# Layer 0's attention heads: masks added by VectorE, two banks for turned blocks, value products in the ring of pairs

## The reference, cut to what matters

```python
content = jnp.einsum('bihd,bjhd->bhij', q + u_bias, k)
pos = jnp.einsum('bihd,jhd->bhij', q + v_bias, p)
pos = _relative_shift(pos)
attn = jax.nn.softmax((content + pos) * scale, axis=-1)
head = jnp.einsum('bhij,bjhd->bihd', attn, v).reshape(B, S, Dm)
```

## Time and profile before

| what | value |
|---|---|
| median of 3 runs | 2649.91 us (2646.68 to 2653.76) |
| the profiled execution | 2652.1 us, its span 2650.3 us |
| setup and projections | 0 to 235 us of the span |
| layer 0's heads | 235 to 1376 us |
| layer 0's merge and experts | 1376 to 2086 us |
| layer 1's heads | 2086 to 2476 us |
| tail | 2476 us to the end |
| share of the span busy | PE 86%, PEld 50%, DVE 61%, ACT 50%, POOL 27% |

### The profile page before, as it was taken

How to read it: one execution, slowest core, us unless ns; L and a number is a source line. 1 busy time by engine, 2 the same in 40 slices (tenths; PEclk the granted TensorE clock), 3 DMA queues, 4 the chain that set the end, 5 groups by cost and what they waited for, 6 DMA issues and landing times. The chain is left out here.

```text
span 2650.3 us, 51680 instructions
## 1 busy us (share of the span) xinstructions
PE 2286.8 (86%) x17274; PEld 1338.0 (50%) x17274; DVE 1618.7 (61%) x2775; ACT 1324.9 (50%) x2282; POOL 704.4 (27%) x573
## 2 busy tenths in 40 slices
PE   3663999999999999999975999999999299999577
PEld 2331777777777777777742444444444144444232
DVE  3894777777777777777744243443442478888354
ACT  1220666566666565656642454455544055555454
POOL 1444444444444444443401122212222100000000
PEclk9775999999999999999986999999999599999799
DMA  4443111111111111111102112122211222222221
GB/s 167 141 143 108 31 37 37 37 37 37 36 33 33 34 33 33 37 37 37 33 22 67 60 40 76 60 87 87 79 36 64 69 72 84 83 83 75 86 77 40
DMA packets 94926, 163.61 MB, mean 62 GB/s; under 512 B 18120, under 2 KB 44242, under 8 KB 93586
## 3 DMA queue, kind: packets, MB, share of 16 engines
q1 hardware_dynamic: 94866, 162.82, 19.5%
HBM read 102.37 MB, written 60.41 MB: 61 GB/s over the span
## 5 line engine op out<-in xcount | busy, mean ns | idle before, releaser
L1112 ACT ACTIVATE prob<-pair,neg_max_h 128x640 f32<-128x640 f32 x512 | 407.0, 795 | 391.0 <-DVE neg_max_h L1012 391.0
L1012 DVE TENSOR_REDUCE neg_max_h<-pair 128x1 f32<-128x640 f32 x512 | 419.5, 819 | 276.2 <-PE pair L936 271.1
L889 PE MATMUL turn<-ident,prob 128*128 128x128 f32 x2048 | 504.9, 278 | 16.1 <-ACT prob_t L1120 9.0
L889 PEld LDWEIGHTS turn<-ident,prob 128*128 128x128 f32 x2048 | 287.3, 140 | 125.5 <-issue 95.6
L1120 ACT COPY prob_t<-turn 128x512 f32<-128x512 f32 x512 | 297.7, 581 | 95.6 <-PE turn L889 93.9
L1588 PE MATMUL pair<-hid,down_w 128*128 128x512 f32 x640 | 307.1, 626 | 29.4 <-DVE moe L1373 25.2
L1072 POOL TENSOR_TENSOR a_full<-rot_c,rot_s 128x512 f32<-128x512 f32 x128 | 162.5, 1269 | 613.0 <-DVE rot_s L1002 613.0
L1891 ACT ACTIVATE prob_h<-pair 128x256 f32<-128x256 f32 (+3 forms) x512 | 205.7, 436 | 195.2 <-PE pair L1778 188.5
L1514 ACT ACTIVATE hid<-pair,up_b 128x512 f32<-128x512 f32 x320 | 200.8, 690 | 124.9 <-PE pair L1568 124.6
L1019 DVE TENSOR_TENSOR prob<-prob 128x128 f32<-128x128 f32 x512 | 256.7, 501 | 0.7 <-ACT prob L1112 0.7
L1830 DVE TENSOR_REDUCE row_max<-pair 128x1 f32<-128x128 f32 (+3 forms) x512 | 221.4, 485 | 56.4 <-PE pair L1757 52.0
(11 more groups left out here) (265 smaller groups left out, 4322.6 us busy)
## 6 DMA issues: line engine op xcount, KB each, us to landing
vx_d<-vx SPq DMA_DIRECT2D x16, 1024.0 KB, 4.8
o_d<-out_sb SPq DMA_DIRECT2D x64, 256.0 KB, 2.0
w_all<-w_d SPq DMA_DIRECT2D x8, 2048.0 KB, 7.1
val<-vx_d SPq DMA_DIRECT2D x32, 256.0 KB, 6.6
val_h<-vx_d SPq DMA_DIRECT2D x32, 256.0 KB
qs_d<-part_q SPq DMA_DIRECT2D x48, 128.0 KB
ks_d<-part_k SPq DMA_DIRECT2D x48, 128.0 KB
num<-o_d SPq DMA_DIRECT2D x24, 256.0 KB
```

Of the source, the lines that this page charges most:

```text
L889: return nc.tensor.transpose(turn_bank[:, jb * P:(jb + 1) * P], prob[s % 4][:, c0:c0 + P], ident[:, :])
L1012: nc.vector.tensor_reduce(neg_max[par][:, s:s + 1], pair[:, S - (ib + 1) * P:2 * S - ib * P], AX_X, ALU.max, negate=True).then_inc(max_don ...
L1112: nc.scalar.activation(prob[s % 4][:, :], pair[:, S - (ib + 1) * P:2 * S - ib * P], ACT.Exp, bias=neg_max[par][:, s:s + 1]).then_inc(exp_d ...
```

## The change

- The two mask products per unit go away. A table `pair_mask` (128 x 1024 in f32, zero but for the masks) is built once in setup, by a memset and two copies on DVE. `dve_max` becomes one fused operation, `tensor_tensor_reduce`: it adds the mask to the 640 scores, negates the sum, writes it to `prob` in SBUF, and takes the minimum of the negated sums into `neg_max`. In the program it is two instructions, the main one and one that writes the 128 x 1 result. It waits for `turned` of four units before as well, since it overwrites that tile.
- `act_exp` reads `prob` in SBUF and writes it in place, with scale -1, in place of reading the pair.
- A pair of scores is free when the fused operation is done (`max_done`), no longer when exp is.
- Turned blocks alternate between `turn_bank` and `out_bank` (`turns`); PE turns unit s once unit s-2 is copied.
- The value products of a query block take a place in the ring of pairs (`PV_SLOTS` = 3, 7, 11, 15), and DVE copies each block's 128 columns on their own (`dve_out`), in place of one copy of 512. Their place is free when that copy is done (`out_copied`). The last two rotations move one slot later (slots 9 and 12). The ring has 24 places in place of 21 (of which 20 were used).

```diff
-            ROT_SLOTS = (2, 5, 8, 11)
+            ROT_SLOTS = (2, 5, 9, 12)
+            PV_SLOTS = (3, 7, 11, 15)
...
-            RING = 21
+            RING = 24
...
                 if kind == "score":
-                    pe.wait_ge(exp_done.sem, exp_done.at(UNITS0 * group + n + 1))
+                    pe.wait_ge(max_done.sem, max_done.at(UNITS0 * group + n + 1))
+                elif kind == "pv":
+                    owner = group - 1 if n == NB - 1 else group
+                    pe.wait_ge(out_copied.sem, out_copied.at(NB * owner + n + 1))
...
-                return nc.tensor.transpose(turn_bank[:, jb * P:(jb + 1) * P], prob[s % 4][:, c0:c0 + P], ident[:, :])
+                return nc.tensor.transpose(turns[s % 2][:, jb * P:(jb + 1) * P], prob[s % 4][:, c0:c0 + P], ident[:, :])
...
-                pe.wait_ge(kept.sem, kept.at(UNITS0 * g + s))
+                pe.wait_ge(kept.sem, kept.at(UNITS0 * g + s - 1))
...
-                nc.tensor.matmul(pair[:, S - P:S], identb[:, :], mask_low, start=False, stop=True, skip_group_check=True)
-                n_up = P + 1 if ib < NB - 1 else P
-                nc.tensor.matmul(pair[:, S:S + n_up], identb[:, :], mask_up[:, 0:n_up], start=False, stop=True,
-                                 skip_group_check=True).then_inc(score_ready.sem, 1)
...
-                nc.vector.tensor_reduce(neg_max[par][:, s:s + 1], pair[:, S - (ib + 1) * P:2 * S - ib * P], AX_X,
-                                        ALU.max, negate=True).then_inc(max_done.sem, 1)
+                v.wait_ge(turned.sem, turned.at(UNITS0 * g + s - 3))
+                v.sem_inc(scores_seen, 1)
+                cols = slice(S - (ib + 1) * P, 2 * S - ib * P)
+                nc.vector.tensor_tensor_reduce(prob[s % 4][:, :], pair[:, cols], pair_mask[:, cols], -1.0, 3.0e38,
+                                               ALU.add, ALU.min, neg_max[par][:, s:s + 1]).then_inc(max_done.sem, 1)
...
-                nc.vector.tensor_copy(out_sb[:, :], out_bank[:, :]).then_inc(out_copied.sem, 1)
+                nc.vector.tensor_copy(out_sb[:, ib * P:(ib + 1) * P], pair[:, 0:P]).then_inc(out_copied.sem, 1)
...
-                nc.scalar.activation(prob[s % 4][:, :], pair[:, S - (ib + 1) * P:2 * S - ib * P], ACT.Exp,
-                                     bias=neg_max[par][:, s:s + 1]).then_inc(exp_done.sem, 1)
+                nc.scalar.activation(prob[s % 4][:, :], prob[s % 4][:, :], ACT.Exp, bias=neg_max[par][:, s:s + 1],
+                                     scale=-1.0).then_inc(exp_done.sem, 1)
```

More of the change, by code:

```diff
@@ L143, in build @@
         out_bank = ctx.enter_context(nc.psum_tensor("outsum", [P, S], F32))
+        turns = [turn_bank, out_bank]
         bank = [pairs[i // 2][:, (i % 2) * S:(i % 2 + 1) * S] for i in range(6)] + [turn_bank, out_bank]
@@ L870, in pair_free @@
                         break
+                    if kind == "pv" and not (n == NB - 1 and first(group)):
+                        break
                     at -= 3
                 if kind == "score":
-                    pe.wait_ge(exp_done.sem, exp_done.at(UNITS0 * group + n + 1))
+                    pe.wait_ge(max_done.sem, max_done.at(UNITS0 * group + n + 1))
+                elif kind == "pv":
+                    owner = group - 1 if n == NB - 1 else group
+                    pe.wait_ge(out_copied.sem, out_copied.at(NB * owner + n + 1))
                 else:
@@ L931, in pe_unit @@
                     turn_block(gt, st, 3).then_inc(turned.sem, 1)
[L932 to L937 removed]
+                nc.tensor.matmul(lo_ap, lo_low, pe_hi[:, S:S + low], start=False, stop=True, skip_group_check=True)
+                nc.tensor.matmul(up_ap, lo_up, pe_hi[:, i0:S], start=False, stop=True, skip_group_check=True
+                                 ).then_inc(score_ready.sem, 1)
             def pe_turn(pe, g, s):
@@ L956, in pe_pv @@
                     pe.wait_ge(val_loaded[par].sem, val_loaded[par].at(16 * (r + 1)))
-                    pe.wait_ge(out_copied.sem, out_copied.at(g))
                 for jb in range(NB):
                     for h in range(GH):
-                        mm = nc.tensor.matmul(out_bank[32 * h:32 * h + 32, ib * P:(ib + 1) * P], val[par][:, jb, h, :],
+                        mm = nc.tensor.matmul(pair[32 * h:32 * h + 32, 0:P], val[par][:, jb, h, :],
                                               prob_t[ib % 2][:, h, jb, :], start=(jb == 0), stop=(jb == NB - 1),
@@ L972, in pe_group @@
                         pe_rotate(pe, *nxt, h, pairs[idx % 3])
[L973 to L976, removed]
+                    if s in PV_SLOTS and not (first(g) and s < GH):
+                        ib = (PV_SLOTS.index(s) - 1) % NB
+                        idx = place["pv", ib]
+                        pair_free(pe, g, idx, nxt is not None)
+                        if ib == NB - 1:
+                            pe_pv(pe, g - 1, r - 1 if par == 0 else r, 1 - par, ib, pairs[idx % 3])
+                        else:
+                            pe_pv(pe, g, r, par, ib, pairs[idx % 3])
             def pe_all(pe):
@@ L993, in pe_all @@
                 pe_turn_max(pe, NG - 1, 1, pairs[0])
-                pe_pv(pe, NG - 1, NG // 2 - 1, 1, NB - 1)
+                pe.wait_ge(max_done.sem, max_done.at(UNITS0 * NG))
+                pe_pv(pe, NG - 1, NG // 2 - 1, 1, NB - 1, pairs[1])
             def dve_rotation(v, n, h, pair):
@@ L1040, in dve_group @@
                         dve_diag(v, gd, sd)
-                    if t == LAG + 1 and not first(g):
-                        dve_out(v, g - 1)
                     if t in ROT_SLOTS and nxt is not None:
@@ L1045, in dve_group @@
                         dve_rotation(v, nxt, h, pairs[place["rot", h] % 3])
+                    if t in PV_SLOTS and not (first(g) and t < GH):
+                        ib = (PV_SLOTS.index(t) - 1) % NB
+                        dve_out(v, g - 1 if ib == NB - 1 else g, ib, pairs[place["pv", ib] % 3])
             def dve_all(v):
@@ L1119, in act_keep @@
                 act.wait_ge(pv_done.sem, pv_done.at(NB * g + ib - 1))
-                nc.scalar.copy(prob_t[ib % 2][:, h].rearrange("p b n -> p (b n)"), turn_bank[:, :]).then_inc(kept.sem, 1)
+                nc.scalar.copy(prob_t[ib % 2][:, h].rearrange("p b n -> p (b n)"), turns[s % 2][:, :]).then_inc(kept.sem, 1)
             def act_group(act, g, par):
```

26 lines of the change are left out of this document (16 added, 10 removed).

## The result

The changed kernel takes 2528.61 us (median of 4 runs, 2522.06 to 2532.69), the kernel before 2651.01 us in the runs beside it: a ratio of 0.9545, 95% interval 0.9526 to 0.9563, or 122 us less. The forecast was 2540 us and 110 us less, in a range of 2518 to 2600. The profiled execution took 2532.68 us, 119.4 less than that of before.

A forecast was written before the change was run, and what follows sets the result against it. TensorE's list with stalls at the turn bank was taken as the bound. Per group 1.76 (masks) + 1.9 (stalls) - 0.2 (new stall) = 3.47 us, x 32 = 111, less 1.5 setup: 110 us gained, 2540 us; range 2518 to 2600.

The forecast's parts named there:

- The bound: Layer 0's heads: TensorE's list sets the pace, 34.7 us per group of 16 units, 1.9 of it stalls at the turn bank.
- Rival B: Turned blocks on TensorE: the stall isn't the bank's, so only the mask products go; 2595 us, chance 0.09.
- The masks: Mask products on TensorE: 0.11 us per unit, 1.76 per group, all on the path; 56 us gained.
- the earlier release: Ring of score pairs: a pair is free some 0.9 us earlier, at the fused operation's end; no gain counted.
- The fused operation: VectorE: main part 0.73 us like the reduction, 0.94 with its second instruction, not slowed beside POOL.
- rival A: VectorE: the fused operation meets GpSimd or its pair costs more than 0.94 us; 2580 us, chance 0.13.
- The read-out: VectorE: the second instruction, 128 x 1, costs between nothing and 0.21 us; 0.21 was taken.
- mostly used: VectorE's load per group rises from about 24 to 27.6 us in 31.0, using most of the slack that hid its order.
- Rival C: VectorE: the fused operation needs two cycles per column, 0.67 us more per unit; slower, 2765 us, chance 0.09.
- What is late next: Slot 12's rotation makes a diagonal late for the turn in unit 15; 0.2 us per group lost again.
- The store: VectorE's copy in slot 7 waits for the previous group's output store, which lands at 11.4 us against 14.0; 2.6 us cover.
- Setup: VectorE's setup gets a memset of 1024 columns and 257 copied ones; 1.5 us, charged in full.

## Why the prediction was right, point by point

*The bound.* TensorE's list plus the stall at the turn bank. Shown: with the bank and the ring alone the idle time before the turns falls to 1 us and the time by 66 us, where 61 were forecast, and with one bank put back the changed kernel loses 91.5. Rival B is out.

*The masks, 56 us*, "all of it on the path", and *the earlier release*, which was costed at nothing by itself. The forecast of the whole is right because next to nothing holds TensorE's list up once all the edits are in: a unit does take 1.55 us. As prices of the parts the terms fail. With one bank the masks bring nothing, even with the earlier release, since the turns still wait for the one bank. Behind the second bank and with pairs released by exp they bring 26 us, since the scores then wait for exps; the earlier release brings the other 28. So in the order bank, masks, release the parts are 66, 26 and 28 us, where 61, 56 and 0 were named: a mis-sized pair of terms whose sum, 54 for 56, is right. The value products' places in the ring also draw on what the release gives; how much was not separated. Rival B's price of 2595, masks gone and the stall kept, was wrong on the same ground: that kernel takes 2653.

*The fused operation.* 819 ns, as the nearest rows had it, and never stretched beside POOL, so that rival A is out. The read-out was taken at its upper end, 0.21 us, and costs 0.02; VectorE's list is 27.6 - 16 x 0.19 = 24.6 us per group, plus 0.5 for the diagonals (532 ns in the mean, 501 before). Its busy time is 828.54 / 32 = 25.9 us per group, where some 28 were named as a sign. The slack was not "mostly used", and a further 5.4 us per group showed it.

*Rival C* was the right danger: one more pass of the same length makes the kernel slower than before. Its 2765 was for 0.67 us more per unit; the second pass, some 0.75, gave 2778. The Trainium skill ("DVE: opcode table, instruction layouts, handler registers and perf-mode slots", § 6 Datapath and trigger behaviour) tells a stage that reads its own last result, without bubbles, from one that routes a result back. The 819 ns for 640 columns agree with the first case.

*What is late next.* 0.2 us per group in unit 15 were forecast; 0.17 were seen, and slot 13 for the rotation took them back.

*The store* is the step that failed outright: "0.6 to issue and 2.0 to land", with 2.6 us of cover. The 2.0 stands on a row that puts 64 stores of both layers together. Asked by line, the trace of the kernel before has a time to landing for layer 1's 32 stores (`L1731`) alone, and none for those of layer 0 (`L829`):

```profile
DMA to landing us min/median/max: 2.0/2.0/2.4
```

So no row showed a store of this place. There the load of the values is issued some 0.8 us behind it, and the copy could start only 7.3 us behind the store's issue. The wait came, 1.06 us in the group shown, and what kept it off the path was luck as far as the prediction goes: a second cover that it didn't name, the rotation in slot 9.

*Setup.* VectorE's added work took what was forecast (the cast of `pe_hi` follows the last mask cast by 1.52 us in place of 0.06), but in these two executions the first score product of the heads starts at 257.11 us, before 257.47, with the inputs 0.47 us earlier. The 1.5 us, charged in full, are at most in part on the path.

*What is left.* Terms gave 3.47 us per group; it is 3.66. Units of 1.54 us in the two middle query blocks make 0.08 of the difference and the smaller stall 0.03; the rest was not traced. 116.9 us lie between the first unit and the last; the rest up to 119.4 is the start and the heads' end, where the last turns wait less for copies.

## What to carry to other kernels

A list of work and the cycle of a buffer (write, hand over, copy, hand over) are two bounds. Shortening the list brings nothing while the buffer's cycle is the longer, so price each edit with the other undone as well as done. The pairs of the ring are such a buffer as well as the turn bank: what releases a place earlier is a term of its own, here half of what seemed to be the masks'. For a transfer that something will wait for, take its duration where it is issued and look what is issued just behind it; a median over all places hides that. And where TensorE has to wait, look at its granted clock in the windows after the wait: with the store issued later the wait was about half of its price.

## What the runs showed of the hardware that was not expected

A read-out of 75 to 85 ns behind a fused operation doesn't hold up the next one: 0.75 us from start to start, within 0.02 of the plain reduction's 0.73. An exp over 640 columns takes 831 ns in the mean when it reads SBUF and 795 in the kernel before, when it reads PSUM; ScalarE's idle time hides it. Two transfers of 256 KB issued 0.8 us apart took 6.6 us (the load) and up to 7.3 (the store), and the load by itself 2.6.
